# Masking the second score pass: a GpSimd select on the exponentials instead of mask matmuls, and sequences written out instead of looped

## The chip, the core and the metric

One core of one Trainium2 chip runs the whole program in one launch. The metric is the device time of one execution in microseconds (us), from the runtime, as the median over executions. The engines are PE (TensorE, the matrix engine), ACT (ScalarE), DVE (VectorE), POOL (GpSimd) and SP (SyncE, which only issues DMAs here). PEld is TensorE's weight load, which the profile lists apart.

## What is computed

Four transformer layers over x, 16 sequences of 256 tokens with 128 features. Each layer is an attention and a feed-forward block, each followed by a residual and a layer norm. The part that the change touches is the causal attention of the first three layers, 16 heads of 8 features each:

```python
# layer 0 (rotary, softmax), layer 1 (latent keys and values, softmax)
scores = einsum('bhqd,bhkd->bhqk', q, k) / sqrt(8)
scores = where(causal, scores, -inf)      # causal: key <= query
attn = softmax(scores, axis=-1)
out = einsum('bhqk,bhkd->bhqd', attn, v)
# layer 2 (no softmax)
attn = where(causal, sigmoid(scores * 4.0), 0.0)
```

The other blocks are two mixtures of experts (layers 0 and 2), a channel mix (layer 1), a linear attention and an MLP (layer 3).

## The kernel before

The program is eight stages one after the other: rope attention, experts 0, latent attention, channel mix, sigmoid attention, experts 2, linear attention, MLP. Every stage walks the 16 sequences. Each engine has its own instruction queue, written out by hand, and all hand-over is by semaphores. A `step(k)` on each engine holds the work of sequence k, mixed with the first part of sequence k+1 ("front": transposes, projections, q and k) and the last part of sequence k-1 ("tail": context, output, layer norm). `pipeline` (L59) runs steps 0, 1, 2 written out, then steps 3 to 14 as an engine loop `Fori` of six iterations of two steps, then step 15 and the last tail. In the loop semaphores are waited for against register values.

In an attention stage the scores of 16 heads are made in six slots, n = 0..5. A slot is 128 partitions x 1024 fp32 in PSUM, and there are two of them (`c.S[:, n % 2]`). Slots n = 0, 1, 3, 4 ("u < 2") hold scores of the diagonal 128x128 tiles and of the tiles beside them, slots 2 and 5 hold diagonal tiles only. `score_slot` (L352) first writes the mask into the diagonal tiles by matmuls with an identity (L360: two of 256 columns in bf16; L363 in slots 2 and 5: two of 512 columns) and then adds the scores on top (L374, fp32 with 32 rows).

- Pass 1 (rope and latent only): the scores with queries in the partitions, masked by `mask_q`; DVE takes the row maxima (L845, L848), and TensorE turns them round (L402, "maxima"). DVE adds them to the queries (L869, `QM`).
- Pass 2 (all three): the scores with keys in the partitions, masked by `mask_k`; ACT turns slot n into `probs[:, n]` in SBUF (L658, `weights`: Exp, or Tanh in the sigmoid stage). `pass2(n)` waits for `probs` n-2, which frees its PSUM slot.
- `weighted(0)` (L444, L448) multiplies probs 0, 1, 2 with the values, `weighted(1)` probs 3, 4, 5. ACT copies the result out (L665).

TensorE's order in the second half of a rope step is: maxima, projections of k+1 (L329), pass2(0), pass2(1), output of k-1 (L482), pass2(2), pass2(3), stack(k+1, 0) (L348, L349: copies of q), weighted(0), pass2(4), stack(k+1, 1) (the same for k), pass2(5), pass1(k+1, 0), pass1(k+1, 1), weighted(1). stack(k+1, 1) waits for DVE's copy `QS` (L834) of what stack(k+1, 0) made. pass1(k+1, 1) waits for probs 5. The latent stage has the same order. The sigmoid stage has no pass 1: there pass2(k+1, 0), which waits for ACT's copy `KS` (L651), stands ahead of weighted(1). ACT's order ends with exp 4, KS, exp 5 in all three.

POOL has little to do: per step it copies x into `xin` (L230), keeps the residual input `xres` (L238 or L240), and makes the layer norm's reciprocal root in `norm_rstd` (L177, L181). DVE writes the normed x after it (L188). In a latent step that write stands ahead of the copy `QS` in DVE's queue, in a rope step behind it.

## Time and profile before

| | |
|---|---|
| median of 2 executions | 2117.7 us (2111.77 and 2123.63) |
| span of the profiled execution | 2108.2 us, 45695 instructions |
| TensorE busy | 1909.0 us, 91% |
| VectorE busy | 1224.0 us, 58% |
| ScalarE busy | 789.7 us, 37% |
| GpSimd busy | 226.6 us, 11% |

The span runs from the first to the last instruction of one profiled execution. The timeline view merges repeats of one group; its times are us from the span's start. Matmuls overlap in it (their ends are modelled), so what one costs is read from start to start. PEclk is the clock that TensorE was granted: 1.00 is 2.4 GHz and 0.50 is 1.2 GHz, and a stretch between them was spent partly at each.

### The profile page before, as it was taken

How to read it: one execution, taken by the hardware profiler on the slowest of the kernel's cores; microseconds unless marked ns; L12 is line 12 of the kernel's file. 1: busy time of each engine (PE TensorE's matmuls, PEld its weight loads, DVE VectorE, ACT ScalarE, POOL GpSimd, SP SyncE). 2: the span in 40 equal slices, each digit the busy share in tenths (PEclk: the TensorE clock that was granted, in tenths of full speed). 3: DMA queues.
4: the chain of work that ended last, by engine and by line, in shares of the span. 5: the costliest groups of instructions: out<-in, count | busy, mean ns of one | idle time of the engine just before them, and what ended most of it. 6: DMA issues, size and time to landing. Idle time of an engine off the chain costs nothing.

```text
span 2108.2 us, 45695 instructions
## 1 busy us (share of the span) xinstructions
PE 1909.0 (91%) x15552; PEld 1501.3 (71%) x15552; DVE 1224.0 (58%) x3651; ACT 789.7 (37%) x1458; POOL 226.6 (11%) x500
## 2 busy tenths in 40 slices
PE   5999999789999999799999999976799979999878
PEld 3666666489999999655666666654566669999667
DVE  4677667556666666455555554548344446666657
ACT  1433443422223232123323323234466645554333
POOL 0000010000000000001001000103111110100234
PEclk9999999789999999868767677678799989999989
DMA  7000000000000000000000000000000000000001
GB/s 236 2 1 0 0 0 0 1 1 1 1 0 0 0 0 0 1 1 1 1 0 0 0 0 0 0 1 0 1 1 0 0 1 2 0 0 0 1 4 36
DMA packets 12191, 15.55 MB, mean 7 GB/s; under 512 B 2944, under 2 KB 10064, under 8 KB 11472
## 3 DMA queue, kind: packets, MB, share of 16 engines
q1 hardware_dynamic: 12112, 14.51, 2.1%
q8 instruction: 48, 0.79, 0.2%
q14 instruction: 31, 0.25, 0.0%
HBM read 12.41 MB, written 2.10 MB: 7 GB/s over the span
## 4 chain that ended last, share of the span: by engine, by line
PE 76%; DVE 11%; issue 6%; ACT 5%; POOL 1%; DVEq 1%; DMA 0%; SPq 0%; ACTq 0%; POOLq 0%
PE O L1633 16%; PE S L374 9%; PE O L444 5%; PE S L1615 5%; PE S L1617 4%; PE S L1616 4%; PE A L329 4%; PE S L360 4%; PE A L348 4%; PE S L363 3%; PE A L349 3%; DVE nm L848 2%; PE O L448 2%; ACT probs L658 2%; PE O L402 2%
## 5 line engine op out<-in xcount | busy, mean ns | idle before, releaser
L1633 PE MATMUL O<-ew,probs 128*128 128x128 f32 x3072 | 386.9, 276 | 1.7 <-ACT probs L1701 1.2
L658 ACT ACTIVATE probs<-S 128x1024 f32<-128x1024 f32 x288 | 290.9, 1026 | 250.1 <-PE S L374 244.4
L1633 PEld LDWEIGHTS O<-ew,probs 128*128 128x128 f32 x3072 | 364.3, 192 | 6.5 <-issue 3.8
L1701 ACT ACTIVATE probs<-S,eb 128x256 f32<-128x256 f32 x512 | 215.2, 472 | 400.5 <-PE S L1617 400.5
L1617 PE MATMUL S<-hi,ew_lo 128*128 128x256 f32 x768 | 217.0, 283 | 0.0
L845 DVE TENSOR_REDUCE nm<-S 128x4 f32<-128x1024 f32 x128 | 150.8, 1217 | 101.7 <-PE S L374 101.6
L1848 DVE SCALAR_TENSOR_TENSOR probs<-O,sc,probs 128x128 f32<-128x128 f32 x448 | 136.6, 346 | 120.1 <-PE O L1633 102.3
L177 POOL TENSOR_TENSOR ve<-mv,eps 128x2 f32<-128x2 f32 x128 | 30.6, 239 | 1551.1 <-DVE mv L169 1551.1
L1615 PE MATMUL S<-hi,QS 128*128 128x256 f32 x512 | 162.8, 318 | 0.0
L1831 DVE TENSOR_SCALAR probs<-S,eb 128x256 f32<-128x256 f32 x256 | 112.0, 479 | 74.7 <-PE S L1617 74.7
L1617 PEld LDWEIGHTS S<-hi,ew_lo 128*128 128x128 f32 x768 | 146.6, 191 | 0.0
L1616 PE MATMUL S<-lo,QS 128*128 128x256 f32 x512 | 145.4, 284 | 0.0
L374 PEld LDWEIGHTS S<-QM,KS 32*128 32x128 f32 x1024 | 88.6, 226 | 71.8 <-issue 71.8
L188 DVE TENSOR_SCALAR X<-res,mv,rstd 128x128 f32 (+1 forms) x256 | 94.4, 410 | 74.7 <-POOL rstd L181 74.5
L444 PE MATMUL O<-probs,V 128*32 128x256 f32 x1536 | 133.8, 423 | 3.8 <-ACT probs L658 3.4
L348 PE MATMUL A<-hi,spread 128*128 128x256 f32 x384 | 119.8, 339 | 17.3 <-DVE lo L824 12.8
L665 ACT COPY OT<-O 128x512 f32<-128x512 f32 x96 | 56.3, 587 | 207.4 <-PE O L448 207.4
L374 PE MATMUL S<-QM,KS 32*128 32x256 f32 (+1 forms) x1024 | 129.3, 358 | 0.0
L374 PEld LDWEIGHTS S<-KS,QS 32*128 32x128 f32 x1024 | 76.8, 198 | 59.8 <-issue 59.8
L834 DVE CAST QS<-A 128x1024 fp32r<-128x1024 f32 x48 | 58.8, 1224 | 94.0 <-PE A L349 94.0
L374 PE MATMUL S<-KS,QS 32*128 32x256 f32 (+1 forms) x1024 | 113.2, 322 | 0.0
L349 PE MATMUL A<-lo,spread 128*128 128x256 f32 x384 | 108.3, 309 | 0.0
(256 smaller groups left out, 3426.9 us busy)
## 6 DMA issues: line engine op xcount, KB each, us to landing
ew<-in_w SPq DMA_DIRECT2D x2, 2048.0 KB
ew<-in_w SPq DMA_DIRECT2D x2, 1024.0 KB
out<-X SPq DMA_DIRECT2D x16, 128.0 KB, 1.8
probs<-in_spread SPq DMA_DIRECT2D x1, 1024.0 KB, 5.1
trig<-in_trig SPq DMA_DIRECT2D x1, 512.0 KB, 6.5
w<-in_w SPq DMA_DIRECT2D x2, 256.0 KB, 4.7
wqk<-in_wqk SPq DMA_DIRECT2D x1, 256.0 KB, 6.4
X<-in_x SPq DMA_DIRECT2D x1, 256.0 KB, 6.7
```

Of the source, the lines that this page charges most:

```text
L348: pe.matmul(out, c.spread[:, 2 * j, g, :], c.hi[:, j, :], start=True, stop=False)
L349: mm = pe.matmul(out, c.spread[:, 2 * j + 1, g, :], c.lo[:, j, :], start=False, stop=True)
L374: mm = pe.matmul(slot[:, b, n * width:(n + 1) * width], lhs[rows, g, tile * P:(tile + 1) * P], right, start=False, stop=True, skip_group_c ...
L444: pe.matmul(c.O[g * ROWS:(g + 1) * ROWS, pr, b * L:(b + 1) * L], c.V[:, par, 0, 4 * g + r, :], c.probs[:, 3 * pr + g // 2, b, 2 * (g % 2): ...
L658: act.activation(c.probs[:, n].rearrange("p b g l -> p b (g l)"), c.S[:, n % 2], ACT.Exp if soft else ACT.Tanh, scale=self.scale).then_inc ...
L845: dve.tensor_reduce(c.nm[:, 1, 2 * pr:2 * pr + 2, 2 * u:2 * u + 2], slot.rearrange("p b (g k) -> p b g k", g=2), AX.X, ALU.max, negate=Tru ...
L1615: pe.matmul(out, self.w1_hi[x][:, chunk], c.hi[:, par], start=True, stop=False)
L1616: pe.matmul(out, self.w1_hi[x][:, chunk], c.lo[:, par], start=False, stop=False)
L1617: mm = pe.matmul(out, self.w1_lo[x][:, chunk], c.hi[:, par], start=False, stop=True)
L1633: mm = pe.matmul(c.O[:, x % 2, t * P:(t + 1) * P], w["h"][:, x % 2, j, t * P:(t + 1) * P], w["w2"][:, x * NJ + j], start=j == 0, stop=j == ...
L1701: act.activation(w["h"][:, x % 2, j], c.S[:, x % 2, bank, col:col + L], ACT.Relu, bias=w["b1"][:, x * self.NJ + j:x * self.NJ + j + 1]).th ...
L1848: ins = dve.scalar_tensor_tensor(dst[:, t, :], c.O[:, x % 2, t * P:(t + 1) * P], w["sc"][:, par, t, x:x + 1], src[:, t, :], ALU.mult, ALU.add)
```

## The change

Pass 2 no longer gets mask matmuls: `score_slot` is called without a mask and its score matmuls start their own accumulation. The constant `mask_k` is gone. Instead POOL runs an `affine_select` in place on each `probs[:, n]` after ACT has written it: key index <= query index keeps the value, otherwise it becomes 0 (-1 in the sigmoid stage, where the value is a tanh). For n = 0, 1, 3, 4 it covers the diagonal tiles (4 x 128 columns), for n = 2 and 5 all 1024 columns. `weighted` waits for the new semaphore `masked` where it waited for `probs`. Pass 1 keeps its matmul masks. Besides, `pipeline` writes out all 16 steps of every stage.

```diff
     front(0, 0)
-    step(0, 0, None, front)
-
-    step(1, 1, tail, front)
-    step(2, 0, tail, front)
-    with eng.Fori(1, (B - 2) // 2) as i:
-        step(2 * i + 1, 1, tail, front)
-        step(2 * i + 2, 0, tail, front)
-    step(B - 1, 1, tail, None)
-    tail(B - 1, 1)
+    for k in range(B):
+        step(k, k % 2, tail if k > 0 else None, front if k < B - 1 else None)
+    tail(B - 1, (B - 1) % 2)
...
+        def mask(s, n):
+            pool.wait_ge(e["probs"].sem, e["probs"].at(s, n + 1))
+            fill = 0.0 if self.kind != "sigmoid" else -1.0
+            if n % 3 < 2:
+                block = c.probs[:, n].rearrange("p b (g t) q -> p b g t q", t=T)[:, :, :, 0, :]
+                pool.affine_select(block, block, [[0, 2], [0, 2], [1, P]], ALU.is_ge, fill, base=0,
+                                   channel_multiplier=-1).then_inc(e["masked"].sem, 1)
+            else:
+                block = c.probs[:, n]
+                pool.affine_select(block, block, [[0, 2], [0, G], [1, P]], ALU.is_ge, fill, base=0,
+                                   channel_multiplier=-1).then_inc(e["masked"].sem, 1)
...
             if has_tail:
-                tail(k - 1, 1 - par)
+                keep(k - 1)
+            for n in range(4):
+                mask(k, n)
+            if has_tail:
+                norm_rstd(c, e, pool, k - 1)
+            mask(k, 4)
+            mask(k, 5)
...
-            for b in range(2):
+            for b in range(2) if mask is not None else ():
...
-                                   start=False, stop=True, skip_group_check=True)
+                                   start=mask is None, stop=True, skip_group_check=True)
...
-            score_slot(c.S[:, n % 2], k, q, pr, u, c.mask_k, 0).then_inc(e["p2"].sem, 1)
+            score_slot(c.S[:, n % 2], k, q, pr, u, None, 0).then_inc(e["p2"].sem, 1)
...
-            pe.wait_ge(e["probs"].sem, e["probs"].at(s, 3 * pr + 3))
+            pe.wait_ge(e["masked"].sem, e["masked"].at(s, 3 * pr + 3))
```

`keep` is the old `tail` on POOL without its `norm_rstd`.

POOL's queue in one inner step of the latent stage before (L247 and L251 belong to the latent norm of k+1, L177 and L181 to the layer norm of k-1):

```order
L230 COPY xin<-X 128x256
L59 ISA
L247 TENSOR_TENSOR lve<-lmv,eps 128x2 [waits lmv,constants_made]
L59 REGISTER_ALU
L251 TENSOR_TENSOR lrstd<-lve,minus_half 128x2 [waits lve,constants_made]
L59 REGISTER_ALU
L240 ISA [waits res,constants_made]
L240 COPY xres<-X 128x256
L59 ISA
L177 TENSOR_TENSOR ve<-mv,eps 128x2 [waits mv,constants_made]
L181 TENSOR_TENSOR rstd<-ve,minus_half 128x2 [waits ve,constants_made]
```

and in the changed kernel, the same step:

```order
L223 COPY xin<-X 128x256 [waits xt_ps,constants_made]
L255 TENSOR_TENSOR lve<-lmv,eps 128x2 [waits lmv,constants_made]
L259 TENSOR_TENSOR lrstd<-lve,minus_half 128x2 [waits lve,constants_made]
L245 COPY xres<-X 128x256 [waits res,constants_made]
L230 AFFINE_SELECT probs<-probs 128x4x128 [waits probs] x2
L234 AFFINE_SELECT probs<-probs 128x1024 [waits probs]
L230 AFFINE_SELECT probs<-probs 128x4x128 [waits probs]
L170 TENSOR_TENSOR ve<-mv,eps 128x2 [waits mv,constants_made]
L174 TENSOR_TENSOR rstd<-ve,minus_half 128x2 [waits ve,constants_made]
L230 AFFINE_SELECT probs<-probs 128x4x128 [waits probs]
L234 AFFINE_SELECT probs<-probs 128x1024 [waits probs]
```

Six selects came in; four of them now stand ahead of the layer norm of k-1, two behind it, and the register instructions of the loop are gone. The steps of the other two attention stages change in the same way.

TensorE's queue in a rope step before, from pass2(0) to pass2(3):

```order
L360 MATMUL S<-mask_k,ident_b 128x2x128 [waits rmax,qm]
L360 MATMUL S<-mask_k,ident_b 128x2x128
L374 MATMUL S<-QM,KS 128x256 x4
L482 MATMUL O<-wo,ctxT 128x128 [waits qm,ctxt]
L482 MATMUL O<-wo,ctxT 128x128
L363 MATMUL S<-mask_k,ident_b 128x512 [waits probs]
L363 MATMUL S<-mask_k,ident_b 128x512
L374 MATMUL S<-QM,KS 128x128 x8
```

and in the changed kernel at the end of a rope step, from pass2(5) to weighted(1):

```order
L388 MATMUL S<-QM,KS 128x128 [waits probs]
L388 MATMUL S<-QM,KS 128x128 x7
L374 MATMUL S<-mask_q,ident_b 128x2x128 [waits probs,ks,qs]
L374 MATMUL S<-mask_q,ident_b 128x2x128
L388 MATMUL S<-KS,QS 128x256 x4
L374 MATMUL S<-mask_q,ident_b 128x2x128 [waits probs]
L374 MATMUL S<-mask_q,ident_b 128x2x128
L388 MATMUL S<-KS,QS 128x256 x4
L458 MATMUL O<-probs,V 32x256 [waits masked]
```

In the first piece the rows with `mask_k` are those that go. In the second, weighted(1) waits for `masked`; before it waited for `probs` at the same place.

## Rows read from the trace of the kernel before

**Rows 1.** The page: span, and TensorE's granted clock in 40 slices
```profile
span 2108.2 us, 45695 instructions
...
PEclk9999999789999999868767677678799989999989
```

**Rows 2.** Windows: stretch, us, busy us of PE, PEld, DVE, ACT, POOL, PEclk, DMA
```profile
131.30:359.50 228.20, 212.87 (x2044) 143.20 (x2041) 160.68 (x301) 92.18 (x120) 19.82 (x40) 1.00 0.00 0
1535.50:1677.00 141.50, 136.44 (x1544) 94.68 (x1540) 61.04 (x176) 97.81 (x121) 18.06 (x44) 1.00 0.00 0
973.10:999.20 26.10, 23.87 (x211) 15.74 (x211) 17.14 (x40) 9.77 (x13) 2.79 (x6) 0.92 0.01 2
1031.70:1355.80 324.10, 304.39 (x2100) 198.38 (x2100) 174.92 (x400) 98.58 (x130) 27.84 (x60) 0.71 0.00 0
1056.20:1059.60 3.40, 1.89 (x15) 0.91 (x12) 3.39 (x10) 0.22 (x1) 0.73 (x2) 1.00 0.00 0
```

**Rows 3.** Timeline, TensorE: a mask and its scores in pass2(2) and pass2(3), rope
```profile
325.50 0.59 PE L363 MATMUL S<-mask_k,ident_b 128*128 128x512 bf16 x2
326.02 0.66 PE L374 MATMUL S<-QM,KS 32*128 32x128 f32 x8
...
326.62 0.39 PE L360 MATMUL S<-mask_k,ident_b 128*128 128x256 bf16 x2
...
326.94 0.50 PE L374 MATMUL S<-QM,KS 32*128 32x256 f32 x4
```

**Rows 4.** One line each (min/median/max ns): GpSimd's copy, two-input add, small add
```profile
L230 POOL COPY xin<-X x48: 397/398/403, 13.5 to 1674.5; 128x256 f32 x36, 128x256 f32<-128x256 f32 x12
...
L238 POOL TENSOR_TENSOR xres<-X,bo x16: 724/777/779, 20.1 to 397.2; 128x256 f32<-128x256 f32 x16
...
L177 POOL TENSOR_TENSOR ve<-mv,eps x128: 195/197/522, 80.7 to 2104.1; 128x2 f32<-128x2 f32 x128
```

**Rows 5.** Timeline, a rope step from the sum of the rotated halves to weighted(0)
```profile
325.25 0.69 DVE L807 TENSOR_TENSOR rot<-t 128x512 f32<-128x512 f32 x1
...
326.73 1.94 ACT L658 ACTIVATE probs<-S 128x1024 f32<-128x1024 f32 x2
...
328.84 0.64 PE L444 MATMUL O<-probs,V 128*32 128x256 f32 x8
```

**Rows 6.** Timeline, the end of that step: exp 5, pass1(k+1, 1), weighted(1)
```profile
333.31 1.02 ACT L658 ACTIVATE probs<-S 128x1024 f32<-128x1024 f32 x1
...
335.14 0.64 PE L444 MATMUL O<-probs,V 128*32 128x256 f32 x8
```

**Rows 7.** Timeline, a sigmoid step: exps 1 and 2, weighted(0), exp 5, weighted(1)
```profile
1576.49 1.99 ACT L658 ACTIVATE probs<-S 128x1024 f32<-128x1024 f32 x2
...
1579.97 0.64 PE L444 MATMUL O<-probs,V 128*32 128x256 f32 x8
...
1584.43 1.02 ACT L658 ACTIVATE probs<-S 128x1024 f32<-128x1024 f32 x1
...
1585.58 0.64 PE L444 MATMUL O<-probs,V 128*32 128x256 f32 x8
```

**Rows 8.** Timeline, a latent step at full clock: exps 2 and 3, norm, QS, stack(k+1, 1)
```profile
978.93 1.94 ACT L658 ACTIVATE probs<-S 128x1024 f32<-128x1024 f32 x2
979.05 0.69 DVE L824 TENSOR_TENSOR lo<-rot,hi 128x512 fp32r<-128x512 f32 x1
...
979.28 0.52 POOL L177 TENSOR_TENSOR ve<-mv,eps 128x2 f32<-128x2 f32 x1 [9.45 <-DVE mv L169]
...
981.24 1.21 DVE L834 CAST QS<-A 128x1024 fp32r<-128x1024 f32 x1
...
983.13 0.38 PE L348 MATMUL A<-hi,spread 128*128 128x256 f32 x1
```

**Rows 9.** Timeline, TensorE: starts of two rope steps that are written out already
```profile
85.86 0.44 PE L280 MATMUL A<-ident,xin 128*128 128x128 f32 x2
108.42 0.44 PE L280 MATMUL A<-ident,xin 128*128 128x128 f32 x2
```

More of the change, by code:

```diff
@@ L99, in __init__ @@
         self.mask_q = sb("mask_q", [P, P], BF16)
-        self.mask_k = sb("mask_k", [P, P], BF16)
         self.ones = sb("ones", [P, P])
@@ L202, in __init__ @@
         ev = dict(xin=1, xt_ps=1, xt=1, v_ps=1, v=T, hi=1, lo=1, qst_ps=1, qs=1, kst_ps=1, ks=1,
-                  p2=6, probs=6, pv=2, ot=2, ctx_ps=1, ctx=2, out_ps=1, xres=1, **LN_EVENTS)
+                  p2=6, probs=6, masked=6, pv=2, ot=2, ctx_ps=1, ctx=2, out_ps=1, xres=1, **LN_EVENTS)
         if kind == "sigmoid":
@@ L230, in front, with keep @@
             pool.tensor_copy(c.xin[:, par], c.X[:, s]).then_inc(e["xin"].sem, 1)
-        def tail(s, par):
+        def mask(s, n):
[9 more added lines that the diff above has]
+                                   channel_multiplier=-1).then_inc(e["masked"].sem, 1)
+        def keep(s):
             if begun(s - 1):
@@ L240, in tail @@
                 pool.tensor_copy(c.xres[:], c.X[:, s]).then_inc(e["xres"].sem, 1)
+        def tail(s, par):
+            keep(s)
             norm_rstd(c, e, pool, s)
@@ L2001, in build @@
                   ("l3", LinearAttention(c, "linear3", w3)), ("l3", Mlp(c, "mlp3", w4, out))]
-        N_MADE = 13
+        N_MADE = 12
         phases[0][1].rest = loaded["x"], 16 * len(loads["x"])
```

1 line of the change is left out of this document (removed).

## The prediction

> **What bounds the kernel now.** I read the page first, then windows by stage, then the timeline of one step of each attention stage, always asking which wait ends last. The profiled span is 2108.2 us [rows 1], 9.5 us under the median of 2117.7; I sum against the span and carry the difference over. The changed stages are the rope stage (an inner step takes 228.20 / 10 = 22.82 us), the latent stage (324.10 / 10 = 32.4 us) and the sigmoid stage (141.50 / 11 = 12.86 us) [rows 2]. TensorE's matmuls cover nearly all of a step, 212.87 of 228.20 us and 136.44 of 141.50 us in the first two windows, and its clock is 1.00 there. The latent stage is another case: PEclk is 0.71, so it runs at 1.2 GHz for (1 - 0.71) / 0.5 = 58% of its time. One latent step ran at 0.92 and took only 26.1 us. The slices of the page show the same dip [rows 1]. So TensorE sets the pace, but with ScalarE close behind it in pass 2: a step ends with exp 5, and weighted(1) starts 0.81 us after exp 5 ends in the rope stage (335.14 against 334.33) [rows 6] and 0.13 us after it in the sigmoid stage (1585.58 against 1585.45) [rows 7].
>
> **What is removed.** A pair of 256-column masks costs TensorE 326.94 - 326.62 = 0.32 us from start to start, a pair of 512-column masks 326.02 - 325.50 = 0.52 us [rows 3]. A sequence has four of the one and two of the other, 2.3 us, and 48 sequences 112 us. That is the most it could bring. Little of it lies on the path: pass2(2) to pass2(5) wait for ScalarE's exps two slots back, which take 0.97 us each when back to back (1.94 for two) [rows 5].
>
> **What a select costs.** The trace has no select. The nearest rows are GpSimd's copy of 256 columns, 0.40 us, the two-input add of 256 columns, 0.78 us, and an add of 2 columns, 0.20 us [rows 4]. That gives 0.2 us fixed and 0.8 ns a column for one input, 2.3 ns for two. A select over 1024 columns then takes between 1.0 and 2.5 us. It reads one operand like the copy, but has to form an index and compare it too, so I take 1.5 us, and 0.85 us for 512 columns. The Trainium skill (GPSIMD Engine Reference, section 3.1) has bodies that compare and then select at 1.03 to 2.03 cycles per element of a 1.2 GHz clock; by that a 1024-column select would be an estimated 0.9 to 1.7 us before its fixed cost, and the sum would come out near mine. No run here shows it yet. To this comes a semaphore hand-over ahead of the select and one behind it, 0.1 us each (exp 5 to weighted(1) takes 0.13 us in the sigmoid stage) [rows 7].
>
> **Rope.** Exps 0 and 1 come up to 0.3 us earlier, but exp 2 stands behind ScalarE's rounding of `rot`, whose sum ends at 325.94 on VectorE, which the masks never delayed. So exp 2 moves from 326.73 to about 326.60 and ends at 327.62 [rows 5]. Its select ends at 327.62 + 0.2 + 1.5 = 329.32, against 328.84 for weighted(0) before: +0.5 us. At the end, TensorE saves 0.32 us in pass2(4), so exp 5 ends 0.32 us earlier relative to weighted(0). Its select then gives weighted(1) at 334.01 + 0.2 + 1.5 = 335.71 against 335.14: +0.6 us [rows 6]. Third, the select of probs 0 (from 325.1) meets `rot` (from 325.25), which has two SBUF inputs [rows 5]. The trace shows such meetings: GpSimd's small add, 0.197 us in the median, takes 0.52 us when it meets VectorE's `lo` [rows 4, 8]. Bounds are 0 and what is left of the select then, 0.7 us; I take 0.4. The Trainium skill (SBUF — State Buffer, "Who interferes with whom") calls this an exclusive lock that is held for the whole instruction; by it the sum would take 0.7 for 0.4, 5 us more in all. Sum 1.5 us a step, over 15 steps 22 us. With the bounds of the select it is 0 to 3.8 us a step.
>
> **Sigmoid.** Here ScalarE runs without a break from the start of a step to the end of exp 2, at 1576.49 + 1.99 = 1578.48, so the missing masks move nothing there [rows 7]. weighted(0) goes from 1579.97 to 1578.48 + 0.2 + 1.5 = 1580.18: +0.2 us. From weighted(0) to weighted(1) it was 5.61 us. This path stays on ScalarE (copy out, exp 4, KS, exp 5), which gains some 0.1 us, and weighted(1) came 0.13 us after exp 5 and now comes 0.2 + 1.5 us after it: +1.5 us. Sum 1.7 us a step, 25 us in all; 10 us with the short select and 55 us with the long one. A select that cost below 0.7 us would be needed to break even.
>
> **Latent.** GpSimd's reciprocal root of k-1 now stands behind selects 0 to 3, VectorE's write of X behind that, and its copy QS behind that, for which stack(k+1, 1) waits. At full clock exp 3 ends at 980.87 before and some 0.5 us earlier now; select 2 ends near 981.0, select 3 near 981.9, root and X together take 981.24 - 979.28 = 1.96 us, QS 1.21 us: 985.1 against 982.45 before [rows 8]. The stack starts at 985.3 against 983.13, +2.2 us, and weighted(1) loses about another 0.9 us. At half clock the picture turns: the four mask pairs ahead of weighted(0), 3 x 0.32 + 0.52 = 1.5 us at full clock [rows 3], cost at most twice as much, TensorE is the slow one there, and I estimate 2 us on the path, which with cover for the root cancels the delays. With 58% of the time at half clock I put the balance at +1 us a step, 15 us; bounds -2 and +4 us.
>
> **Loops.** The rope steps that are written out already take 108.42 - 85.86 = 22.56 us, those in the loop 22.82 us [rows 9, 2]: 0.26 us, over 12 steps 3 us. For the other seven stages the bounds are 0 and the same 0.26 us, 22 us in all; I take 4. Together -7 us. The Trainium skill (Runtime: NRT & Kernel Launch, "Instruction fetch mechanics") has a taken branch out of the two resident pages stall until the target is fetched; the loop steps here show only the 0.26 us. By the page the gain would be larger, by the rows it is 7 us.
>
> **The clock.** This is the largest term and the least certain. The latent stage shows what brings the clock down: in the 3.4 us before it falls at 1059.7, matmuls cover 1.89 us [rows 2]. The rope and sigmoid steps have no such stretch now. After the change they get one: behind pass2(5) TensorE waits for KS, makes one slot, waits for exp 5 and then for its select. In the sigmoid step that is about 3.7 us with 0.45 us of matmuls, in the rope step 3.6 us with 1.5 us. So I expect 1.2 GHz for part of nearly every step. Price from rows: the usual latent step has 0.58 x 32.4 = 18.8 us at half clock, the fast one 0.16 x 26.1 = 4.2 us, and they differ by 6.3 us: 0.43 us for each us at half clock [rows 2]. Estimating 6 us of it per rope step and 5 us per sigmoid step gives 2.6 and 2.1 us, together 15 x 4.7 = 70 us.
>
> **Sum.** 22 + 25 + 15 - 7 + 70 = +125 us: a span of 2233 us and a median of 2243 us.
>
> **Rivals.** (1) The waits come, the clock stays up. For it: only the latent stage falls today, and VectorE stalls TensorE in rope steps too. Then +55 us, 2173 us, still slower by over 2%. (2) A short select, 1.0 us, and no clock drop: rope 0, sigmoid +10, latent about +5, loops -7: +8 us, 2126 us. (3) Faster: a select so short that it hides. It decides from 0.6 us for 1024 columns, at which weighted(1) in the rope stage no longer waits (0.81 less the two hand-overs). Rope then gains 0.4 us a step, sigmoid 0.8, latent 1.3, with the loops 45 us: 2073 us. Against it: a copy at 0.8 ns a column is longer. (4) Faster by the clock: shorter half-clock stretches let the latent stage run like its fast step, 15 x 6.3 = 94 us, against +40 elsewhere: 2064 us. (5) A select far slower than 2.5 us: GpSimd, idle for most of the time, then becomes the bound in the sigmoid stage (4096 columns a step: 2.4 ns each plus its 2.9 us of small work fill 12.8 us). At 4 us for 1024 columns rope and sigmoid lose 6.5 us a step each, latent about 5 us: with loops and clock 2117.7 + 270 - 7 + 70 = 2451 us.
>
> **Chances.** Forecast 0.66; (1) 0.12; (2) 0.11; (3) 0.04; (4) 0.03; (5) 0.04. Faster by over 2% (2% is about what a measurement of this kernel can tell from no change): 0.07; within: 0.11; slower: 0.82. The low end of the range, 2130, is the short select with a small clock loss; the high end, 2350, is the long select (rope 57, sigmoid 55, latent 45) with the clock term.
>
> **What would show it.** Right: selects of 1 to 2 us on GpSimd; weighted(1) released by GpSimd in all three stages; PEclk under 1.00 in the rope and sigmoid stages; in the latent stage QS after X, after a late root. Wrong: PEclk at 1.00 in the rope stage takes 40 us off; weighted released by ScalarE or nothing; a latent PEclk well above 0.71; a sigmoid step under 13 us.

## The result, and the profile after

The changed kernel takes 2150.6 us (median of 2 runs, 2140.3 to 2160.9) against 2117.7 us: a ratio of 1.016, interval 1.009 to 1.023. It is slower, but by 33 us where 125 were forecast; whether by as much as 2% the interval leaves open, and the two runs lie 20 us apart. Its profiled span is 2138.6 us, 30.4 us over that of before [rows 1].

The page: the span, the busy times, the granted clock in 40 slices (to be held against [rows 1]), the two groups of selects and the first weighted matmuls.
```profile
span 2138.6 us, 40821 instructions
...
PE 1846.9 (86%) x14976; PEld 1504.8 (70%) x14976; DVE 1225.4 (57%) x3650; ACT 781.5 (37%) x1458; POOL 446.6 (21%) x788
...
PEclk7898888869999999957777777767887859999999
...
L230 POOL TENSOR_SCALAR_AFFINE_SELECT probs<-probs 128x512 f32<-128x512 f32 x192 | 124.8, 650 | 540.9 <-ACT probs L672 539.4
...
L458 PE MATMUL O<-probs,V 128*32 128x256 f32 x1536 | 166.3, 517 | 47.3 <-POOL probs L234 47.2
...
L234 POOL TENSOR_SCALAR_AFFINE_SELECT probs<-probs 128x1024 f32<-128x1024 f32 x96 | 105.0, 1094 | 109.6 <-ACT probs L672 109.6
```
A select takes 1.09 us for 1024 columns and 0.65 us for 512. TensorE's weighted matmuls now wait for it, 47.2 us in all. The first seven slices (the rope stage) read 7898888 for 9999999, and slices 30 to 32 (the sigmoid stage) 878 for 999.

Windows of ten inner steps in the rope, latent and sigmoid stage (columns as in [rows 2]); before, a step took 22.82, 32.4 and 12.86 us [rows 2].
```profile
156.45:410.30 253.85, 217.56 (x1914) 150.46 (x1913) 162.46 (x301) 91.60 (x120) 67.39 (x100) 0.87 0.01 1
1071.56:1363.39 291.83, 253.20 (x1984) 180.92 (x1980) 170.57 (x401) 96.77 (x130) 71.08 (x120) 0.76 0.00 1
1557.35:1716.97 159.62, 134.46 (x1280) 96.82 (x1280) 58.84 (x160) 87.94 (x111) 62.75 (x100) 0.78 0.01 1
```
The rope step went to 25.4 us and the sigmoid step to 16.0 us, with the clock at 0.87 and 0.78 where it was 1.00. The latent step went the other way, to 29.2 us. Three stages, two signs: that is where the forecast has to be taken apart.

Timeline of the changed kernel, a rope step, from the first select to the stack of k+1 (start, length, instruction, in brackets the idle time before it and its releaser).
```profile
325.89 0.64 POOL L230 TENSOR_SCALAR_AFFINE_SELECT probs<-probs 128x512 f32<-128x512 f32 x1 [13.07 <-ACT probs L672]
325.95 1.11 DVE L821 TENSOR_TENSOR rot<-t 128x512 f32<-128x512 f32 x1
326.80 0.77 POOL L230 TENSOR_SCALAR_AFFINE_SELECT probs<-probs 128x512 f32<-128x512 f32 x1 [0.27 <-ACT probs L672]
327.10 0.62 ACT L658 CAST hi<-rot 128x512 fp32r<-128x512 f32 x1 [0.37 <-DVE rot L821]
...
328.55 0.55 PE L362 MATMUL A<-hi,spread 128*128 128x256 f32 x1 [1.26 <-ACT hi L658]
```
`rot` takes 1.11 us where it took 0.69 [rows 5], since the select of probs 0 runs beside it. ScalarE's `hi` is late by that much, and TensorE stands still for 1.26 us ahead of the stack. The end of the same step:
```profile
335.17 1.01 ACT L672 ACTIVATE probs<-S 128x1024 f32<-128x1024 f32 x1
...
336.25 1.09 POOL L234 TENSOR_SCALAR_AFFINE_SELECT probs<-probs 128x1024 f32<-128x1024 f32 x1 [1.39 <-ACT probs L672]
...
337.40 0.64 PE L458 MATMUL O<-probs,V 128*32 128x256 f32 x8 [0.33 <-POOL probs L234]
```
From the end of exp 5 (336.18) to weighted(1) it is 1.22 us, against 0.81 before [rows 6]. In the sigmoid stage it was 0.13 us [rows 7] and is now 1.29 us, with a longer stall (1.60 us) and at half clock (the same eight matmuls take 1.08 us, not 0.64):
```profile
1604.08 1.01 ACT L672 ACTIVATE probs<-S 128x1024 f32<-128x1024 f32 x1
...
1605.24 1.09 POOL L234 TENSOR_SCALAR_AFFINE_SELECT probs<-probs 128x1024 f32<-128x1024 f32 x1 [0.49 <-ACT probs L672]
...
1606.38 1.08 PE L458 MATMUL O<-probs,V 128*32 128x256 f32 x8 [1.60 <-POOL probs L234]
```

### The profile page after: what moved, and what is told of

Its sections match the earlier page's. It is cut to its first block, busy times and chain, and to the rows that moved or that the text cites. A ratio compares the mean times of both kernels' runs of the same rounds, so it can differ in the third digit from the quotient of the medians.

```text
span 2138.6 us, 40821 instructions
## 1 busy us (share of the span) xinstructions
PE 1846.9 (86%) x14976; PEld 1504.8 (70%) x14976; DVE 1225.4 (57%) x3650; ACT 781.5 (37%) x1458; POOL 446.6 (21%) x788
## 4 chain that ended last, share of the span: by engine, by line
PE 65%; DVE 14%; issue 9%; POOL 6%; ACT 5%; DMA 0%; SPq 0%; POOLq 0%; DVEq 0%; ACTq 0%
PE O L1647 16%; PE O L458 6%; PE S L388 6%; PE S L1629 5%; PE S L1631 4%; PE S L1630 4%; ACT probs L672 4%; POOL probs L234 3%; PE O L462 3%; PE A L343 3%; PE A L362 2%; DVE nm L862 2%; DVE nm L859 2%; PE O L416 2%; PE A L363 2%
## 5 line engine op out<-in xcount | busy, mean ns | idle before, releaser
L672 ACT ACTIVATE probs<-S 128x1024 f32<-128x1024 f32 x288 | 288.0, 1024 | 201.4 <-PE S L388 199.0
L230 POOL TENSOR_SCALAR_AFFINE_SELECT probs<-probs 128x512 f32<-128x512 f32 x192 | 124.8, 650 | 540.9 <-ACT probs L672 539.4
L458 PE MATMUL O<-probs,V 128*32 128x256 f32 x1536 | 166.3, 517 | 47.3 <-POOL probs L234 47.2
L170 POOL TENSOR_TENSOR ve<-mv,eps 128x2 f32<-128x2 f32 x128 | 25.2, 197 | 863.9 <-DVE mv L162 863.9
L362 PE MATMUL A<-hi,spread 128*128 128x256 f32 x384 | 136.0, 373 | 44.6 <-ACT hi L658 17.7
L181 DVE TENSOR_SCALAR X<-res,mv,rstd 128x128 f32<-128x128 f32 x256 | 96.0, 416 | 102.4 <-POOL rstd L174 101.9
L388 PE MATMUL S<-QM,KS 32*128 32x256 f32 (+1 forms) x1024 | 140.4, 374 | 7.6 <-ACT probs L672 7.6
L362 PEld LDWEIGHTS A<-hi,spread 128*128 128x128 f32 x384 | 95.9, 250 | 62.2 <-ACT hi L658 32.1
L388 PEld LDWEIGHTS S<-QM,KS 32*128 32x128 f32 x1024 | 102.3, 240 | 38.7 <-ACT probs L672 15.6
L234 POOL TENSOR_SCALAR_AFFINE_SELECT probs<-probs 128x1024 f32<-128x1024 f32 x96 | 105.0, 1094 | 109.6 <-ACT probs L672 109.6
L363 PE MATMUL A<-lo,spread 128*128 128x256 f32 x384 | 122.8, 340 | 0.0
```

The costliest lines, as they stand in the source:

```text
L234: pool.affine_select(block, block, [[0, 2], [0, G], [1, P]], ALU.is_ge, fill, base=0, channel_multiplier=-1).then_inc(e["masked"].sem, 1)
L362: pe.matmul(out, c.spread[:, 2 * j, g, :], c.hi[:, j, :], start=True, stop=False)
L363: mm = pe.matmul(out, c.spread[:, 2 * j + 1, g, :], c.lo[:, j, :], start=False, stop=True)
L388: mm = pe.matmul(slot[:, b, n * width:(n + 1) * width], lhs[rows, g, tile * P:(tile + 1) * P], right, start=mask is None, stop=True, skip_ ...
L458: pe.matmul(c.O[g * ROWS:(g + 1) * ROWS, pr, b * L:(b + 1) * L], c.V[:, par, 0, 4 * g + r, :], c.probs[:, 3 * pr + g // 2, b, 2 * (g % 2): ...
L672: act.activation(c.probs[:, n].rearrange("p b g l -> p b (g l)"), c.S[:, n % 2], ACT.Exp if soft else ACT.Tanh, scale=self.scale).then_inc ...
```

## The experiments

Each "step" below is the tenth part of a window over ten inner steps of that stage, from the write of X of one sequence to that of the tenth after it. Medians are in us, ratios against the kernel before in the same session (2112 to 2120 us).

| kernel | median | ratio, interval | rope | latent | sigmoid |
|---|---|---|---|---|---|
| before | 2117.7 | | 22.80 | 32.41 | 12.85 |
| changed | 2150.6 | 1.016, 1.009 to 1.023 | 25.39 | 29.18 | 15.96 |
| e1 loops written out only | 2093.6 | 0.988, 0.986 to 0.990 | 22.72 | 31.43 | 12.78 |
| e14 attention written out only | 2107.8 | 0.996, 0.994 to 0.998 | 22.57 | 32.04 | 12.75 |
| e2 select in latent only | 2055.0 | 0.969, 0.967 to 0.971 | 22.72 | 29.24 | 12.75 |
| e3 no masking in pass 2 | 2038.5 | 0.962, 0.960 to 0.963 | 23.35 | 28.32 | 12.33 |
| e8 masks and selects | 2154.6 | 1.019, 1.016 to 1.023 | 23.89 | 32.13 | 14.31 |
| e4 changed, fill rope, sigmoid | 2075.4 | 0.979, 0.977 to 0.981 | 23.29 | 29.31 | 13.41 |
| e5 e2, fill latent | 2028.6 | 0.959, 0.957 to 0.961 | 22.56 | 27.63 | 12.76 |
| e6 e1, fill latent | 2038.0 | 0.963, 0.960 to 0.966 | 22.56 | 28.04 | 12.75 |
| e7 e5, early root | 2027.1 | 0.958, 0.956 to 0.960 | 22.56 | 27.34 | 12.76 |
| e9 short selects, all stages | 2055.1 | 0.973, 0.970 to 0.976 | 23.93 | 28.62 | 12.28 |
| e10 e7, short selects in latent | 1999.0 | 0.945, 0.943 to 0.948 | 22.73 | 25.66 | 12.75 |
| e11 e10, short selects in sigmoid | 2008.3 | 0.948, 0.947 to 0.950 | 22.57 | 25.64 | 13.65 |
| e12 e11, selects 3, 4 in rope | 2007.8 | 0.948, 0.947 to 0.949 | 22.25 | 25.60 | 13.64 |
| e13 e12, early root in latent only | 1983.3 | 0.938, 0.936 to 0.941 | 22.28 | 25.62 | 12.28 |

**The two halves of the change.** e1 takes the new `pipeline` and leaves the masks with TensorE.

> The kernel before with all sequences written out and its mask matmuls kept. Theory A (the loops were worth little): 2111 us, -7 us, latent step still near 32 us with PEclk near 0.71. Rival B (the latent stage got faster because its loop is gone, 32.4 to 29.0 us a step): near 2067 us, latent step near 29 us.

Writing the loops out is worth 27 us of the medians and 20.5 us of the spans (2087.7 against 2108.2), not 7. Rival B fails: the latent step is 31.43 us, so its loop is not what took it to 29. The select by itself therefore costs 2150.6 - 2093.6 = 57 us of the medians, 51 us of the spans. e14 writes out the attention stages alone:

```diff
+def pipeline_flat(eng, front, step, tail): ...   # as pipeline in the changed kernel
-        pipeline(pe, front, {...}[kind], tail)     # in Attention, on all four engines
+        pipeline_flat(pe, front, {...}[kind], tail)
```


> The kernel before with the three attention stages written out and the engine loops kept in the five other stages; masks and all else as before. Reference points: before 2117 us (mix step 4.13 us, moe2 15.17, linear 3.95, latent 32.41), all written out 2093.6 us (3.75, 14.88, 3.61, 31.43). If each stage's loops cost what they cost in that stage: mix, moe2 and linear as before, rope and latent as written out: about 2107 us, some 13 us of the 24 to 27 us staying lost. If unrolling acts through the clock of the attention stages: 2098 us or less. If it acts only in the short stages: 2115 us.

It was 2107.8 us: 8 us less than before, with 14 us left to the other stages. Windows of before, ten inner steps of the mixing stage, the last expert stage and the linear attention:
```profile
1435.44:1476.77 41.33, 26.77 (x118) 19.64 (x116) 34.05 (x117) 16.80 (x46) 15.12 (x30) 0.76 0.00 0
1783.79:1935.54 151.75, 150.11 (x1243) 143.10 (x1242) 96.66 (x451) 76.69 (x200) 15.41 (x39) 1.00 0.00 0
1987.23:2026.70 39.47, 34.70 (x183) 24.76 (x183) 30.37 (x100) 13.98 (x39) 15.90 (x30) 1.00 0.00 0
```
The same of e1:
```profile
1426.11:1463.63 37.52, 22.51 (x115) 17.21 (x113) 33.81 (x118) 16.78 (x45) 15.31 (x30) 0.86 0.00 1
1770.03:1918.83 148.80, 148.79 (x1242) 143.02 (x1242) 96.89 (x451) 76.14 (x200) 15.41 (x39) 1.00 0.01 2
1969.71:2005.80 36.09, 33.29 (x181) 24.19 (x180) 31.46 (x100) 13.37 (x37) 15.89 (x30) 1.00 0.00 1
```
0.38, 0.30 and 0.34 us a step. In e14, which keeps these loops, the three windows took 41.34, 151.97 and 38.33 us. So most of the loops' cost lies where they are. It is not the same everywhere: over ten inner steps the first expert stage took 276.11 us and the MLP 37.33 us in both kernels, and there TensorE was busy for all of the window. In the mixing stage a part may be the clock, 0.76 before and 0.86 in e1. What stays open is the latent stage: its code is the same in e1 and e14, and its step took 31.43 and 32.04 us, with the clock at 0.75 and 0.72.

**Waits or missing matmuls.** e2 leaves the select in the latent stage and gives the other two their masks back; e3 leaves out the masking of pass 2 altogether (its time is that of the kernel without any mask there); e8 has both masks and selects.

```diff
-            score_slot(c.S[:, n % 2], k, q, pr, u, None, 0)...
+            score_slot(c.S[:, n % 2], k, q, pr, u, None if kind in SELECT else c.mask_k, 0)...   # e2
+            score_slot(c.S[:, n % 2], k, q, pr, u, c.mask_k, 0)...                               # e8
```


> All sequences written out; GpSimd's select only in the latent stage, mask matmuls in the rope and sigmoid stages. Theory A (select costs in rope and sigmoid, gains in latent, stages add up): rope step 22.6 us, sigmoid step 12.8 us, both at clock 1.00, latent step 29 us; total 2150 - 40 - 42 = about 2066 us. Rival C (the stages' steps are tied to each other or to the chip's run, so the latent step would not hold): latent step near 32 us, total about 2110 us.

> The changed kernel without its selects: pass 2 is not masked at all, weighted waits for probs as before. Theory A (it is the wait for the select that empties TensorE and lets the clock fall): rope step near 22.5 us and sigmoid step near 12 us with PEclk near 1.00, latent step 27 to 28 us; total near 2020 us. Rival D (it is the missing mask matmuls themselves that let the clock fall): PEclk in the rope stage stays near 0.87 and its step at 24 us or more; total near 2070 us.

> Both at once in all three attention stages: the pass 2 bf16 mask matmuls stay and GpSimd selects as well (no engine loops). It adds the waits without taking matmuls away. Reference points: no select, masks 2093.6 us (rope step 22.72, sigmoid 12.78, latent 31.43; rope stage 53 us at half clock); select instead of masks 2150.6 us (25.38, 15.96, 29.18; 143 us). Theory H (the clock falls partly because 2.3 us of matmuls a sequence are gone): half clock in the rope stage below 100 us, rope step 24 to 24.5, sigmoid step about 15, latent step 32 or more: about 2155 us, the gain of the latent stage being lost. Rival I (the waits alone bring the clock down, the missing matmuls have no part in it): rope step 25.5 or more, sigmoid 16 or more with as much half clock as in the changed kernel, 2190 us.

e2 beats both kernels: 2055.0 us. The select loses in two stages and gains in the third, as theory A had it. e3 came out between its two theories, in the steps and in the total. With nothing to wait for, the sigmoid step is 0.45 us shorter than with masks, but the rope step is 0.63 us longer. Windows of e3, rope stage, and of e8, all three:
```profile
151.91:385.45 233.54, 203.82 (x1926) 142.14 (x1924) 161.10 (x300) 92.11 (x121) 19.04 (x39) 0.94 0.01 1
```
```profile
153.36:392.25 238.89, 220.06 (x2042) 145.99 (x2040) 160.13 (x301) 93.12 (x121) 69.48 (x100) 0.97 0.01 1
1071.54:1392.86 321.32, 294.56 (x2108) 189.19 (x2102) 171.42 (x402) 98.87 (x130) 71.86 (x120) 0.75 0.00 1
1587.38:1730.45 143.07, 127.14 (x1402) 87.75 (x1400) 57.40 (x161) 89.01 (x111) 63.75 (x100) 0.98 0.01 2
```
e8 confirms theory H in the clock. With the waits alone it stays at 0.97 and 0.98, with the matmuls alone gone it is 0.94 in the rope stage (and 0.95 in the sigmoid stage), and with both it is 0.87 and 0.78. Each brings little; the pair brings the fall. The rope and sigmoid steps came out shorter than theory H had them (24 to 24.5 us and about 15). e8 also gives the wait without the clock: rope 23.89 - 22.72 = 1.17 us, sigmoid 14.31 - 12.78 = 1.53 us, latent 0.70 us. And the step from e8 to the changed kernel is what taking 2.3 us of masks away did: rope +1.50, sigmoid +1.65, but latent -2.95 us.

In the rope stage a part of the 1.50 is not the masks' absence alone, as e9 below shows: `rot` came out of the way in e8.

The trace of the changed kernel also shows where the clock falls. Two stretches of its rope step shown above, the last of the wait for `hi` and the stack behind it (columns as in [rows 2]):
```profile
328.20:328.55 0.35, 0.01 (x1) 0.04 (x1) 0.24 (x1) 0.35 (x2) 0.00 (x0) 0.57 0.00 0
328.60:331.40 2.80, 2.80 (x20) 2.12 (x24) 0.77 (x1) 0.96 (x2) 1.68 (x2) 0.50 0.00 0
```
Read on through the ten rope steps, the clock falls fourteen times: ten times in this wait for `hi`, once in every step, and only four times at the end of a step, where pass1(k+1, 1) is still running ahead of the wait for the select. About 50 of the 63 us at half clock follow the wait for `hi`. In the sigmoid step shown above it falls at 1604.9, with exp 5 still running (it ends at 1605.09) and its select not begun. So what the clock fell in was seldom the wait for the select itself.

**What the clock is worth.** e4 is the changed kernel with matmuls whose result nothing reads, in the places where TensorE waits:

```diff
+        def fill(bank, count):
+            for _ in range(count):
+                pe.matmul(bank, c.ident_b[:], c.mask_q[:].unsqueeze(1).broadcast_to((P, G, P)), start=True, stop=True, ...)
...
+                fill_ahead_of_stack(k, 5)        # rope, bank O0, ahead of stack(k + 1, 0)
...
+                pe.wait_ge(e["probs"].sem, e["probs"].at(k, 5))
+                fill(c.S[:, 0, 0], 2)            # ahead of the first slot of k + 1
...
+                fill(c.O[:, 1], FILL_LAST.get(kind, 0))  # weighted(1), ahead of its wait: rope 1, sigmoid 6
+                pe.wait_ge(e["masked"].sem, e["masked"].at(s, 6))
```


> The changed kernel with extra matmuls (512 columns, bf16, results overwritten) in TensorE's waits of the rope stage (5 ahead of stack(k+1,0), 2 ahead of pass1(k+1,0), 1 ahead of weighted(1)) and of the sigmoid stage (2 ahead of pass2(k+1,0), 6 ahead of weighted(1)). Theory A (waits cost about 1 us a step, the rest of the loss is half clock): PEclk 1.00 in both stages, rope step 25.5 to about 23.6 us, sigmoid step 15.9 to about 13.8 us, total near 2090 us. Rival E (the waits themselves are the whole loss, the clock costs little): steps stay at 25 and 15.5 us or grow, total 2145 us or more.

Windows of e4, rope and sigmoid:
```profile
153.36:386.22 232.86, 215.40 (x2001) 143.13 (x2001) 163.47 (x300) 91.60 (x121) 67.19 (x100) 0.99 0.01 1
1528.30:1662.36 134.06, 125.35 (x1362) 84.57 (x1360) 57.45 (x160) 86.24 (x111) 62.14 (x100) 1.00 0.01 2
```
More work made the kernel 75 us faster in the medians, 62 us in the profiled spans. Rival E fails, and both steps came out shorter than theory A had them. The clock is back at 0.99 and 1.00. Per step it gives back 25.39 - 23.29 = 2.10 us in the rope stage and 15.96 - 13.41 = 2.55 us in the sigmoid stage, 70 us if all 15 steps gained as much. What then remains against e1 in these two stages is 0.57 and 0.63 us a step, 18 us: the select's waits less what the missing masks free. The fill itself may hold something up, so 18 us is an upper bound.

e5 and e6 do the same in the latent stage, with the select and with the masks; e7 also moves the reciprocal root ahead of select 2.

```diff
             pass1(k, par, 3)
+            if has_tail:
+                fill(c.O[:, 1], 4)
...
+            if has_tail:
+                fill(c.O[:, 1], 2)
             pass1(k, par, 5)
...
+            if has_tail:
+                fill(c.O[:, 1], 3)
             maxima(k, has_front)
...
+                fill_ahead_of_stack(k, 4)
                 stack(k + 1, 0)
...
+                pe.wait_ge(e["probs"].sem, e["probs"].at(k, 5))
+                fill(c.S[:, 0, 0], 2)
                 pass1(k + 1, nxt, 0)
```


> The select in the latent stage only (bf16 mask matmuls in pass 2 of the rope and sigmoid stages, no engine loops), plus extra matmuls whose result nothing reads, in the five places of a latent step where TensorE waits. Reference points: without the extra matmuls 2055.0 us, latent step 29.24 us with 273 us of the stage at half clock. Theory A (TensorE's clock is what the latent step is long by): the half-clock share falls below a quarter of the stage, the step goes to 26.5 to 27.5 us, 30 to 40 us less in all: about 2020 us. Rival F (the extra matmuls only delay what is queued behind them): the step stays at 29 us or above, 2055 us or more.

> The same extra matmuls in the latent step, but bf16 mask matmuls in pass 2 of all three stages and no select at all (no engine loops). Reference point without the extra matmuls: 2093.6 us, latent step 31.43 us. Theory A: clock up, step 27 to 28 us, 50 to 65 us less: about 2035 us. What the prediction had worked out for full clock (the select makes GpSimd's root, X, QS and with them the second stack late by 2.2 us): then this kernel's step is SHORTER than that of the kernel with the select and the extra matmuls, by 1 to 2 us. Rival G (the select helps in the latent stage at either clock, as the masks are on the path at full clock too): this step is longer than that one by 1 us or more.

```diff
-            for n in range(4):
+            mask(k, 0)
+            mask(k, 1)
+            if has_tail:
+                norm_rstd(c, e, pool, k - 1)
+            for n in range(2, 5):
                 mask(k, n)
-            if has_tail:
-                norm_rstd(c, e, pool, k - 1)
-            mask(k, 4)
             mask(k, 5)
```


> As the kernel with the select in the latent stage and the extra matmuls, but GpSimd computes the reciprocal root of the sequence before ahead of select 2 instead of behind select 3. If the late root is on the path at full clock (the prediction's step): X, QS and the second stack come about 2 us earlier and the latent step is 1 to 2 us shorter, 15 to 30 us in all. If the path goes through pass 2 and weighted(0) and not through the root: the same within 5 us, select 2 being held up by 0.2 us at most.

Windows over ten latent steps, of e5 and of e6:
```profile
1022.39:1298.64 276.25, 261.49 (x2138) 167.57 (x2134) 172.75 (x402) 95.45 (x130) 76.11 (x120) 0.89 0.01 1
```
```profile
1029.91:1310.32 280.41, 276.16 (x2253) 171.75 (x2251) 170.69 (x401) 98.27 (x130) 27.50 (x60) 0.91 0.01 1
```
The fill is worth 3.39 us a step with masks and 1.61 us with selects, so the clock is a large part of the latent step too, though neither came to 1.00. Of the select's lead of 2.19 us at a clock of 0.75 (e1) there are 0.41 us left at 0.9. Neither reading set down for e6 came true: I had wanted the select behind by 1 to 2 us at full clock, rival G ahead by 1 us or more. As no latent step ran at 1.00, my working for full clock is not tested by these two.

e7 moves the root for 0.28 us a step; the medians (2028.6, 2027.1) don't part. It moved less than it was meant to: `QS` begins 0.46 us behind the start of weighted(0) in a step where it began 1.02 us behind it in e5, since the two halves of X now run beside the selects and take 1.69 us for 0.60. What settles it is e5 itself, with the late root, from `QS` to pass2(4) and the second stack:
```profile
1104.58 1.22 DVE L878 CAST QS<-A 128x1024 fp32r<-128x1024 f32 x1
...
1105.67 0.50 PE L394 MATMUL S<-QM,KS 32*128 32x256 f32 x4
...
1106.10 0.38 PE L368 MATMUL A<-hi,spread 128*128 128x256 f32 x1
```
`QS` ends at 1105.80, while pass2(4) is still on TensorE, and the stack follows pass2(4) without a wait. The late root is not on the path in this step; in the ten steps of e5 TensorE waited for `QS` twice, 0.8 us in all, and in the ten of the changed kernel never.

**Which select costs.** In e9 GpSimd keeps the four 512-column selects of a sequence, and the slots that weighted waits for last, 2 and 5, keep their mask matmuls:

```diff
+            score_slot(c.S[:, n % 2], k, q, pr, u, None if kind in SELECT and u < 2 else c.mask_k, 0)...
+            pe.wait_ge(e["masked"].sem, e["masked"].at(s, 2 * pr + 2))      # in weighted
+            pe.wait_ge(e["probs"].sem, e["probs"].at(s, 3 * pr + 3))
```


> All three attention stages: GpSimd selects in the four slots of pass 2 in which only 512 columns have to be masked, and slots 2 and 5, which are the last ones that weighted(0) and weighted(1) wait for, keep their two bf16 mask matmuls and get no select (no engine loops). Theory W (what the rope and sigmoid stages lose begins with weighted waiting for the 1024-column select behind exp 2 and exp 5): nothing waits for a select any more, rope step 22.6 to 23.0 us (22.72 with masks only, 25.38 with selects only), sigmoid step 12.6 to 12.9 (12.78, 15.96), latent step 29.2 to 29.9; about 2060 us. Rival M (taking TensorE's mask matmuls away is enough to bring its clock down, as in the run that left the masks out, 92 us at half clock in the rope stage): rope step 23.2 or more, over 80 us at half clock, about 2075 us.

Windows of e9, rope and sigmoid:
```profile
154.47:393.80 239.33, 212.29 (x1962) 145.59 (x1962) 165.40 (x301) 92.40 (x121) 46.34 (x80) 0.93 0.00 1
1517.61:1640.42 122.81, 113.59 (x1325) 82.48 (x1321) 58.34 (x161) 87.61 (x110) 40.65 (x80) 1.00 0.01 2
```
In the sigmoid stage theory W holds and more: 12.28 us, shorter than with masks. The latent step is shorter too than either reading had it, 28.62 us. In the rope stage theory W fails: 23.93 us, in rival M's range. The groups by line say why, `rot` and the first matmuls of the stacks, of e9:
```profile
L831 DVE TENSOR_TENSOR rot<-t 128x512 f32<-128x512 f32 x10 | 11.1, 1113 | 0.3
...
L370 PE MATMUL A<-hi,spread 128*128 128x256 f32 x80 | 28.8, 377 | 12.6 <-ACT hi L668 12.6
```
of e8:
```profile
L828 DVE TENSOR_TENSOR rot<-t 128x512 f32<-128x512 f32 x10 | 6.9, 692 | 0.3
...
L368 PE MATMUL A<-hi,spread 128*128 128x256 f32 x80 | 21.3, 302 | 2.4 <-issue 2.4
```
and of e3:
```profile
L822 DVE TENSOR_TENSOR rot<-t 128x512 f32<-128x512 f32 x10 | 6.9, 692 | 0.3
...
L363 PE MATMUL A<-hi,spread 128*128 128x256 f32 x80 | 24.0, 329 | 8.4 <-ACT hi L659 8.4
```
Without the masks TensorE comes to the stack 0.84 us before `hi`, and where the select of probs 0 holds `rot` up it stands there for 1.26 us, just as in the changed kernel. The clock of e9 falls there, once in each of the ten steps. In e8 the masks delay exp 0 and its select just enough. Timeline of e8:
```profile
337.62 0.69 DVE L828 TENSOR_TENSOR rot<-t 128x512 f32<-128x512 f32 x1
337.77 1.04 POOL L236 TENSOR_SCALAR_AFFINE_SELECT probs<-probs 128x512 f32<-128x512 f32 x1 [13.56 <-ACT probs L679]
```
Here `rot` begins 0.15 us before the select and takes its usual 0.69 us, and it is the select that takes 1.04 us for 0.64; in the changed kernel the select begins 0.06 us before `rot`, and `rot` pays. Who comes second pays, and of the two TensorE waits only for `rot`. So e12 keeps only selects 3 and 4 in the rope stage. It rests on e10 (e7 with the latent stage's short selects) and e11 (the sigmoid stage's too).

```diff
-SELECT = {'latent': (0, 1, 3, 4), 'sigmoid': (0, 1, 3, 4)}                       # e11
+SELECT = {'rope': (3, 4), 'latent': (0, 1, 3, 4), 'sigmoid': (0, 1, 3, 4)}       # e12
```

> Latent stage only: the four 512-column selects, mask matmuls in slots 2 and 5, the extra matmuls and the early root; rope and sigmoid stages with mask matmuls. Reference point with all six selects: 2027.1 us, latent step 27.34 us. If weighted(1) waiting for the last select matters: it starts about 1 us earlier against 0.5 us more matmuls in slot 5, latent step 0.3 to 0.7 us shorter, about 2020 us. If the mask matmuls of slots 2 and 5 are on the path instead (TensorE at half clock for a third of the stage): 0.3 to 0.8 us longer, about 2035 us.

> The 512-column selects (slots 0, 1, 3, 4) in the latent and sigmoid stages, mask matmuls in slots 2 and 5 there and in all slots of the rope stage, the extra matmuls and the early root in the latent stage, no engine loops. By adding the two stages as measured apart (1999.0 us with the latent part, sigmoid stage 214 us with short selects against 224 us without): about 1990 us, rope step 22.7. If they don't add because the clock of one stage hangs on the one before: 1999 us or more.

> The same, and in the rope stage the select in slots 3 and 4 alone, mask matmuls in slots 0, 1, 2 and 5, so that no select runs while VectorE adds up rot. With short selects in slots 0, 1, 3 and 4 the rope step was 23.93 us with 105 us of the stage at half clock; rot took 1.11 us for 0.69, and TensorE waited for hi ahead of the stack. Theory L (the select of probs 0 that meets rot makes hi and the stack late, and TensorE's clock falls in that wait): rot at 0.69 us, the wait for hi gone, half clock back near 50 us, rope step 22.5 to 22.8 us, the kernel within 5 us of the one without selects in the rope stage. Rival M (it is the missing mask matmuls): half clock 80 us or more, rope step 23.2 or more, 8 us or more above it.

Windows of e12, ten rope steps, and its `rot`:
```profile
148.56:371.01 222.45, 202.75 (x2004) 138.45 (x2000) 162.64 (x301) 91.74 (x121) 31.16 (x61) 1.00 0.01 1
```
```profile
L856 DVE TENSOR_TENSOR rot<-t 128x512 f32<-128x512 f32 x10 | 6.9, 692 | 0.3
```
22.25 us at a clock of 1.00: better than any rope step with masks alone (22.56 to 22.72). Rival M had expected 23.2 or more with the masks of two slots gone. But e12 gives the rope stage two things back at once, `rot` at its usual length and the masks of slots 0 and 1, and so it does not part them. One thing of theory L was wrong: the wait for `hi` did not go, it fell to 7.8 us in ten steps, and the clock stood that. In e3 the clock fell to 0.94 with 8.4 us of the same wait and no masks at all, so the masks have a part in it beside `rot`. The step is 0.32 us shorter than in e11, 5 us over 15 steps, which the medians, 0.6 us apart, do not show (the spans, 2010.8 and 2003.0, do).

e10 did more than it should have: 28 us below e7, the step 1.68 us shorter for the 0.3 to 0.7 expected. Two mask pairs came back and the wait for the last select (3.3 us in ten steps of e7) went, and with them the clock rose from 0.90 to 0.97; which of the two did it stays open.

e11 was to be 1990 us and came out above e10, at 2008.3 us. Its sigmoid step was 13.65 us, where e9 had 12.28 with the same short selects. The timeline at the end of such a step, e11:
```profile
1543.04 0.69 POOL L176 TENSOR_TENSOR rstd<-ve,minus_half 128x2 f32<-128x2 f32 x1
1543.36 1.02 ACT L707 ACTIVATE probs<-S 128x1024 f32<-128x1024 f32 x1
1543.68 1.23 POOL L238 TENSOR_SCALAR_AFFINE_SELECT probs<-probs 128x512 f32<-128x512 f32 x2
...
1544.96 0.64 PE L475 MATMUL O<-probs,V 128*32 128x256 f32 x8 [0.94 <-POOL probs L238]
```
The early root, harmless in the latent stage, stood in all three. In the sigmoid stage VectorE's statistics come late; selects 3 and 4 queue behind the root and both come after it. e13 moves the root back in the rope and sigmoid stages.

```diff
+            early = self.kind == "latent"
+            mask(k, 0)
+            mask(k, 1)
+            if has_tail and early:
+                norm_rstd(c, e, pool, k - 1)
+            mask(k, 2)
+            mask(k, 3)
+            if has_tail and not early:
                 norm_rstd(c, e, pool, k - 1)
             mask(k, 4)
```

> As the kernel of 2007.8 us (short selects in slots 3 and 4 of the rope stage and in 0, 1, 3, 4 of the latent and sigmoid stages, extra matmuls in the latent stage), but the reciprocal root stands ahead of select 3 in the latent stage alone; in the rope and sigmoid stages it is behind select 3 again. Theory Q (in the sigmoid stage the root waits for VectorE's statistics until after exp 5 has begun, and selects 3 and 4 behind it on GpSimd hold weighted(1) up by 0.9 us, which brings the clock down): sigmoid step back to 12.3 us (from 13.64), half clock in that stage about 23 us (from 55), rope and latent unchanged: about 1985 us. Rival K (the clock at the start of the sigmoid stage comes from the stage before, and the root has no part in it): step stays above 13.2 us, 2000 us or more.

Windows of e13, the three stages:
```profile
149.05:371.82 222.77, 203.10 (x2005) 138.71 (x2004) 160.55 (x300) 92.08 (x121) 31.90 (x60) 1.00 0.01 1
1013.97:1270.14 256.17, 244.49 (x2162) 157.88 (x2151) 174.53 (x401) 95.96 (x130) 53.84 (x100) 0.96 0.01 1
1451.25:1574.09 122.84, 113.62 (x1328) 82.51 (x1324) 58.34 (x161) 87.61 (x110) 40.64 (x80) 1.00 0.01 2
```
Theory Q holds: 12.28 us for the 12.3 expected. At 1983.3 us it is 6.2% faster than the kernel before and 7.8% faster than the changed one (1983.3 / 2150.6).

## Why the prediction was wrong

The direction was right, the size was not: +125 us were forecast and +33 came. The sign of the latent term was wrong, the select was priced too high, and the clock term came out to the microsecond in part by luck. The terms side by side, in us over 15 steps:

| term | forecast | measured | from |
|---|---|---|---|
| waits in rope and sigmoid, less what the masks free | +47 | +18 | e4 against e1 |
| clock in rope and sigmoid | +70 | +70 | changed against e4, in steps |
| latent | +15 | -34 | changed against e1, 29.18 - 31.43 |
| loops | -7 | -20.5 (medians -27) | e1 against before |
| sum | +125 | +33.5 (spans +30.4) | |

- **Clock: the sum right, in part by luck.** It was the term I called least certain. I had 2.6 us for the rope step and 2.1 for the sigmoid step; it was 2.10 and 2.55. The time at half clock was 2 x (1 - 0.87) x 25.4 = 6.6 us and 2 x (1 - 0.78) x 16.0 = 7.0 us a step, for 6 and 5, and each of these microseconds cost 0.32 and 0.36 us, for my 0.43: two errors that cancel. The place was only half right. I put the fall down to the new wait at the end of the step, with 0.45 us of matmuls in 3.7 us (sigmoid) and 1.5 in 3.6 (rope); in the steps shown above they were 1.44 and 2.55 us. In the rope stage ten of fourteen falls came in the wait for `hi` instead, which I had counted as a delay and not as a cause of the clock. And e8 shows that the waits alone hardly move the clock while the masks are still there to keep TensorE busy.
- **The latent stage: the sign was wrong.** The step that failed is "I estimate 2 us on the path, which with cover for the root cancels the delays", and with it the balance of +1 us a step: it was -2.25 us. I took only the four mask pairs ahead of weighted(0) and set too much against them. The groups by line over ten latent steps of before, the masks of pass 2, had the number:
```profile
L360 PE MATMUL S<-mask_k,ident_b 128*128 128x256 bf16 x80 | 22.1, 374 | 0.0
...
L363 PE MATMUL S<-mask_k,ident_b 128*128 128x512 bf16 x40 | 16.7, 509 | 0.0
```
  That is 38.8 us in ten steps, 3.9 us of TensorE a step, and three quarters of it was on the path at a clock of 0.75: taking it out gave 2.95 us (e8 against the changed kernel), the waits took 0.70, and the difference is the 2.25 us a step that the stage gained. The late root, which I priced at 2.2 us for full clock, was hardly on the path at a clock of 0.89 (e5, 0.8 us in ten steps), and moving it gave 0.28 us (e7). At full clock it stays untested.
- **The waits: the select priced too high, a saving left out.** The select is 1.09 us for my 1.5. The row of the copy, 0.2 us and 0.8 ns a column, was nearly the price, and what I put on top of it for the index and the comparison was not there. (The bodies that compare and select, which I took from the Trainium skill, stand in the GPSIMD Engine Reference under "7. Performance pitfalls for Q7 kernels" and not in its section 3.1; measured were 0.89 ns a column, an estimated 1.07 of its cycles of 1.2 GHz, near the lower end of 1.03 to 2.03.) With 1.09 us in place of 1.5 my own sums give an estimated 0.7 us a step in the rope stage and 1.1 us in the sigmoid stage, 27 us in place of 47. e4 has at most 18, so the rest is mainly "the missing masks move nothing there", which failed: the waits alone took 1.17 us in the rope stage (e8, where `rot` is not held up) and 1.53 us in the sigmoid stage, the net is 0.57 and 0.63 us (e4, where `rot` is held up), and so the removed matmuls give back 0.6 to 1.0 and about 0.9 us a step. The `rot` term measured 1.11 - 0.69 = 0.42 us for my 0.4, a figure taken between the bounds 0 and 0.7.
- **Loops: the term undersized.** I took the 0.26 us of rope steps as the upper bound for the other stages and put 4 of its 22 us into the sum, for no reason that a row gave. Three stages paid 0.30 to 0.38 us a step, the latent stage 0.98 us, which e1 and e14 leave unexplained. The Trainium skill (Runtime: NRT & Kernel Launch, "Instruction fetch mechanics") has a taken branch out of the resident pages wait for a fetch; no row here shows such a fetch. Nor is there one price per pass: the first expert stage (27.61 us a step) and the MLP (3.73 us) take as long with the loop as without it, and in both TensorE has no gap in the window. What decides between the stages stays open.

Of the rivals, (2), the short select with no clock drop, had the select right and the clock wrong. (4), the latent stage at its fast step's 26.1 us, did not come with this change (29.18 us at 0.76), but e10, with the fill and the short selects, shows that it can be had: 25.66 us at 0.97. The clock rules out (1), and the 1.09 us rule out (3) and (5). The signs I named as telling came out so: weighted(1) is released by GpSimd in all three stages, the clock is under 1.00 in two of them, QS comes after a late root in the third. Of the signs for "wrong" only the latent clock moved, to 0.76, and most of that came with the loops (0.75 in e1).

## What to carry over

Work taken from an engine gains little where another engine's result is what it waits for, and it can lose: TensorE's clock fell where both the matmuls went and a wait came, and filling the waits with matmuls that nothing reads won back some 4.7 us a step over the two stages. Look for the fall in the trace before naming the wait that brings it: here it was mostly another one than the new wait on the select. Before pricing a change by one stage's balance, split the stages by the clock that they run at: 2.3 us of masks (full-clock price) were worth 2.95 us a step where the clock was 0.75, and 0.6 to 1.0 us where it was near 1.00. And where an operation moves to an idle engine, let it do only the pieces that nobody waits for last, keep them from running beside a two-input operation on the path, and look up what stands ahead of them in that engine's queue.
